# Expert weight loads issued by ScalarE instead of SyncE, and the expert tile ahead of the router in the draining steps of a fused perceiver block

## The chip, the core and the metric

One of the eight cores of a Trainium2 chip runs the program. The metric is device time in microseconds (us), of which a median of several runs is given. A profiled execution has a time of its own and a span, which runs from the first to the last instruction that the profiler saw.

## What is computed

The input is x with 64 sequences of 32 tokens and 256 channels, and a context of 64 x 257 x 256, all float32. Three blocks follow each other, each added to x:

```python
x = x + xattn(layernorm(x), ctx, ...)   # attention over the context and the own 32 keys, LoRA weights
x = x + attn(layernorm(x), ...)         # RWKV: a scan over time, then a mixture of 8 experts, top 2
x = x + ffn(layernorm(x), ...)          # GEGLU: one shared expert and 8 experts, top 1

# the mixture of the second block, ei = layernorm of its stream, shifted = ei one token later
probs = softmax(ei @ router_w); top 2 of 8, weights renormalised
xk = ei * mk + shifted * (1 - mk);  xr = ei * mr + shifted * (1 - mr)
out_e = sigmoid(xr @ eWr[e]) * (square(relu(xk @ eWk[e])) @ eWv[e])
```

eWk is 8 x 256 x 512, eWv 8 x 512 x 256, eWr 8 x 256 x 256: 4, 4 and 2 MB.

## The kernel before

The 2048 tokens are cut into G = 16 chunks of 128 (four sequences each). One software pipeline of STEPS = 25 steps, written out by hand, takes the chunks through the cross attention, the time mixing and the routing. In step s the attention works on chunk s, the time mixing begins on chunk s-3, the norm after it and the router's scores are those of chunk g = s-7, and the counting and listing of its tokens by expert is that of chunk s-8 on VectorE and s-9 on GpSimd. Each engine has its own function with its own order of the work inside a step: `mix_sync` (SyncE, only DMAs), `mix_pool` (GpSimd), `mix_tensor`, `mix_scalar` and `mix_vector`. They meet through semaphores alone, and an engine runs its list strictly in order. From step 16 on no attention chunk is left, so the steps get shorter: these are the draining steps.

The mixture of experts works on NT1 = 39 tiles of 128 token places of one expert each. Its first TA = 12 tiles need the lists of the first CUT = 10 chunks alone (`tile_map_a`, lines 1322 to 1347, in step 18), so the mixture begins at step MOE_AT = 20, inside the pipeline: each engine calls `moe(s - MOE_AT)` as the last thing of the steps 20 to 24, and alone after them. For a tile, SyncE fetches the list of its tokens (`moe_pick`, line 336: a DMA of 4 bytes to each of 128 partitions), GpSimd gathers the rows (`gather`, line 347, which waits for that list; the first three gathers stand at the end of step 19), TensorE turns them (`turned`, line 391), ScalarE copies them and the expert's eWk (`copies`, line 451), VectorE mixes (`mixed`, line 529), and TensorE multiplies (`hidden`, `receptance`, `down`). In the steps 20 to 22 the router still has the chunks 13 to 15: `router(g)` of TensorE (line 907), whose scores `router(g)` of ScalarE copies (line 1142) and VectorE's `largest` (line 1293) reads in the step after. On both engines the router stands ahead of the expert tile.

SyncE's list is the longest of the DMA lists. For each chunk `store_normed` (line 577) waits until GpSimd's `normed` (line 738) has the rows, and stores them to HBM by five DMAs: one of 128 rows of 1 KB, and one for each sequence of 31 rows of 1 KB, moved down by one token. Behind the stores of the steps 16, 17 and 18 SyncE issues the expert weights by `load_k`, `load_v` and `load_r` (lines 584 to 595). Their rows are 2 KB for eWk and 1 KB for the others:

| step | issued | rows |
|---|---|---|
| 16 | eWk of experts 0 to 5, eWr of 0 to 5 | 1536, 1536 |
| 17 | eWk of 6 and 7, eWv of 0 to 4 | 512, 2560 |
| 18 | eWv of 5 to 7, eWr of 6 and 7 | 1536, 512 |

Then comes the store of step 19 (chunk 12) and, behind it, `moe_pick` of the first 12 tiles. The weights overwrite the buffers of the attention (`arena_a`, `xz`), hence the waits in front of them. ScalarE's list has DMAs too: the context rows (`load_values`, line 1038) until step 13, and later the experts' results (`store`, line 474).

Of ScalarE's step, the parts on which the change bears are these, in order: `scaled_in`, `norm_out(g)` (line 1098, it feeds TensorE's `normed_T` and GpSimd's `normed`), `exponents`, `norm_T(g)` (line 1104), `copy_in`, `gate_exp` (line 1134), `router(g)` (line 1144), `softmax`, `load_values`, `moe`. Of TensorE's: `keys`, `turned`, `project_mix`, `normed_T(g)` (line 842), `ranks` (lines 977 to 979), `values`, `receptance`, `router(g)` (lines 912 and 914), `moe` (lines 397, 408, 423, 436).

Of the kernel before, what the change touches and what calls it, by code (L numbers as in the profile page):

```python
# [5 lines left out]
P = 128  # L6
# [54 lines left out]
def perceiver_block(nc, x_in, ctx_n, ctx_t, w_att, lora, early_in, late_in, w_mix,  # L61
                    eWk, eWv, eWr, w1s, w2s, w3s, W1, W2, W3, Wg, out):
    BATCH, S, D = x_in.shape
    KD = D // P
# [19 lines left out]
    with cx, nc.allow_non_contiguous_dma(reason="per-channel vectors, one element a partition"):  # L84
# [305 lines left out]
        def moe_tensor(pe):  # L390
# [36 lines left out]
            def down(n):  # L427
                e = pe.value_load(expert1[0:1, n:n + 1], min_val=0, max_val=E - 1)
                if n == 0:
                    pe.wait_ge(dv_ev, G)  # L430
                    pe.wait_ge(ld_moe[3], 16)
                    pe.wait_ge(ld_moe[4], 16)
                pe.wait_ge(m_dsq, n + 1)
                need(pe, m_dy, n)
                for f in range(FKC):
                    last = nc.tensor.matmul(bMY[:, 0:D], hT[:, n % 2, f * P:(f + 1) * P],  # L436
                                            ewv_sb[:, e, f * D:(f + 1) * D], start=f == 0, stop=f == FKC - 1)
                last.then_inc(m_py, 1)
# [11 lines left out]
        def moe_scalar(act):  # L450
            def copies(n):
                if n == 0:
                    act.wait_ge(pe_z, G)
                    act.wait_ge(pe_r, G)
                    act.wait_ge(dv_x1, G)
                    act.wait_ge(ld_moe[2], 16)
                    act.wait_ge(ld_moe[3], 16)
                mapped(act, n)
                act.wait_ge(m_pa, n + 1)
                need(act, m_dx, n - 1)  # L460
                nc.scalar.activation(prevT[:, n % 2], bMT[:, 0:KD * P], ACT.Copy).then_inc(m_ap, 1)
                e = act.value_load(expert1[0:1, n:n + 1], min_val=0, max_val=E - 1)
                need(act, m_ph, n - 1)
                nc.scalar.activation(wk_e[:, n % 2], ewk_sb[:, e], ACT.Copy).then_inc(m_awk, 1)  # L464
# [102 lines left out]
        def mix_sync(sp):  # L567
# [9 lines left out]
            def store_normed(n):  # L577
                sp.wait_ge(po_ei, n + 1)
                sp.dma_start(rows_e[n * P:(n + 1) * P, D:2 * D], ei[:, n % EI]).then_inc(ei_out[n % EI], 16)
                for j in range(BG):  # L580
                    r = n * P + j * S
                    sp.dma_start(rows_e[r + 1:r + S, 0:D], ei[j * S:j * S + S - 1, n % EI]).then_inc(ei_out[n % EI], 16)

            def load_k(lo, hi, i):
                sp.dma_start(ewk_sb[:, lo:hi].rearrange("p e (k f) -> p e k f", k=KD),
                             eWk[lo:hi].rearrange("e (k p) f -> p e k f", p=P)).then_inc(ld_moe[i], 16)

            def load_v(lo, hi, i):
                sp.dma_start(ewv_sb[:, lo:hi].rearrange("p e (k f) -> p e k f", k=FKC),
                             eWv[lo:hi].rearrange("e (k p) f -> p e k f", p=P)).then_inc(ld_moe[i], 16)  # L590

            def load_r(lo, hi, i):
                sp.wait_ge(dv_x1, 2 * hi)
                sp.dma_start(ewr_sb[:, lo:hi].rearrange("p e (k f) -> p e k f", k=KD),
                             eWr[lo:hi].rearrange("e (k p) f -> p e k f", p=P)).then_inc(ld_moe[i], 16)
            load_x(0)
            sp.dma_start(w_T.rearrange("p i k o -> p (i k o)"), w_att).then_inc(ld_w, 16)
            load_keys(0)
# [9 lines left out]
            for s in range(STEPS):  # L608
                n, g = s + N3, live(s - LAG - 4)
                if n in (5, 8):  # L610
                    load_x(3 if n == 5 else 4)
                if n < G:
                    load_keys(n)
                if s == 0:
                    sp.wait_ge(po_mix, 1)
                    sp.dma_start(rows_e.rearrange("(b s) d -> b s d", s=S)[:, 0, 0:D], zero_rows[:]).then_inc(zero_out, 16)
                    sp.dma_start(tab_e.rearrange("(p f) o -> p (f o)", p=P), zero_tab[:]).then_inc(zero_tab_out, 16)
                if g is not None:
                    store_normed(g)
                if s == G:  # L620
                    sp.wait_ge(pe_s, G)
                    load_k(0, 6, 2)
                    load_r(0, 6, 0)
                if s == G + 1:
                    sp.wait_ge(dv_o, G)
                    load_k(6, E, 3)
                    load_v(0, 5, 3)
                if s == G + 2:
                    sp.wait_ge(dv_x1, G)
                    load_v(5, E, 4)  # L630
                    load_r(6, E, 1)
                if s == MOE_AT - 1:
                    moe_pick(sp, range(TA))
            sp.dma_start(r2_w[:], Wg.rearrange("(k p) e -> p k e", p=P)).then_inc(ld_s, 16)
# [163 lines left out]
        def mix_tensor(pe):  # L798
# [192 lines left out]
            for s in range(STEPS):  # L991
# [30 lines left out]
                    scores(a)  # L1022
                if s == LAG - 1:
                    router_bias()
                if g is not None:
                    router(g)
                if s == STEPS - 1:
                    totals()
                if s >= MOE_AT:
                    moe(s - MOE_AT)  # L1030
            for m in range(STEPS - MOE_AT, MSTEPS):
                moe(m)

        def mix_scalar(act):
# [6 lines left out]
            for n in range(N3):  # L1041
                load_values(n)
            nc.scalar.preload_act_table(ACT.Exp)

            def hidden(n):
                act.wait_ge(pe_h, n + 1)
# [101 lines left out]
            for s in range(STEPS):  # L1148
# [23 lines left out]
                    hidden(s + 1)  # L1172
                if s == LAG - 1:
                    router_bias()
                if g is not None:
                    router(g)
                if a is not None:
                    softmax(a)
                if N3 <= s + 2 < G:
                    load_values(s + 2)  # L1180
                if s >= MOE_AT:
                    moe(s - MOE_AT)
            for m in range(STEPS - MOE_AT, MSTEPS):
                moe(m)

# [920 lines left out]
```

## Time and profile before

| | |
|---|---|
| median of 3 runs | 1017.66 us (1012.83 to 1019.77) |
| the profiled execution | 1014.11 us |
| its span | 1012.3 us |
| TensorE, matmuls, busy share of the span | 89% |
| VectorE, ScalarE, GpSimd | 42%, 29%, 31% |
| granted TensorE clock, mean over the span | 0.948 of full |
| pipeline of 25 steps | about 0 to 350 us |

Times in the rows are microseconds from the start of the span. A row of the timeline gives start, duration, engine, line, operation, what it writes from what, the shapes, and in brackets how long the engine was idle before it and what released it. "SPq" and "ACTq" rows are DMA issues of SyncE and ScalarE: their duration is that for which the issuing engine's list was held, not that of the transfer. A released-by in brackets is inferred from semaphores.

### The profile page before, as it was taken

The page shows a single profiled execution, that of the slowest core. Times are in us where ns is not written, and L with a number is a line of the kernel's source. Part 1 is how long each engine was busy: PE and PEld are TensorE (multiplying, and loading weights), DVE is VectorE, ACT ScalarE, POOL GpSimd, SP SyncE. Part 2 cuts the span into 40 slices and gives each one's busy share as a digit, 9 for nine tenths or more (in the row PEclk, how much of TensorE's full clock was granted, in tenths as well). Part 3 has the DMA queues.
Part 4 walks back from the last instruction along what each step waited for, and adds up shares of the span by engine and source line. Part 5 has one row for each costly group of instructions (what it writes and reads, how often), then busy time and mean ns, then how long its engine had stood idle before and what let it go on. Part 6 is the DMA issues. An engine that isn't in the chain of part 4 may idle for free. (4 is left out here: it accounts for less than half of the span.)

```text
span 1012.3 us, 19824 instructions
## 1 busy us (share of the span) xinstructions
PE 898.9 (89%) x6726; PEld 815.5 (81%) x6726; DVE 424.4 (42%) x1173; ACT 294.3 (29%) x665; POOL 308.9 (31%) x547
## 2 busy tenths in 40 slices
PE   5799999999723898999995999995999999999994
PEld 4577787888722788999984999994899999999993
DVE  2346766767842556555542333336111111111113
ACT  1345555545412444544531111110111111111110
POOL 1823456656515422343203322220210100100006
PEclk8899999999875899999997999997999999999998
DMA  9844545652862232325311111110699898899715
GB/s 349 260 176 163 186 121 173 149 118 38 219 216 55 64 77 67 90 85 182 111 43 58 48 32 32 31 47 11 232 347 324 298 330 317 299 310 328 260 59 166
DMA packets 100417, 163.75 MB, mean 162 GB/s; under 512 B 12488, under 2 KB 78664, under 8 KB 98152
## 3 DMA queue, kind: packets, MB, share of 16 engines
q1 hardware_dynamic: 81392, 115.82, 35.6%
q0 software_dynamic: 7552, 19.56, 7.7%
q10 hardware_dynamic: 11392, 27.34, 7.2%
q8 instruction: 46, 0.75, 0.3%
q14 instruction: 35, 0.29, 0.1%
HBM read 146.08 MB, written 16.60 MB: 161 GB/s over the span
## 5 line engine op out<-in xcount | busy, mean ns | idle before, releaser
L1697 PEld LDWEIGHTS bank<-zT_f,we 128*128 128x128 f32 x1472 | 167.9, 192 | 1.9 <-ACT zT_f L1985 0.7
L1697 PE MATMUL bank<-zT_f,we 128*128 128x128 f32 x1472 | 168.2, 275 | 0.5 <-ACT zT_f L1985 0.5
L1714 DVE TENSOR_TENSOR hT_f<-bank,act_g 128x512 f32<-128x512 f32 x78 | 53.8, 691 | 227.9 <-PE bank L1697 208.2
L1706 ACT ACTIVATE act_g<-bank 128x512 f32<-128x512 f32 x78 | 46.6, 597 | 320.8 <-PE bank L1697 320.8
L1697 PE MATMUL bank<-zT_c,a_x 128*128 128x128 f32 x1024 | 121.3, 280 | 0.3 <-PEq L1527 0.3
L1697 PEld LDWEIGHTS bank<-zT_c,a_x 128*128 128x128 f32 x1024 | 119.1, 196 | 0.8 <-issue 0.7
L863 PE MATMUL bank<-arena_b,mixed_w 128*128 128x128 f32 x768 | 94.2, 281 | 0.0
L863 PEld LDWEIGHTS bank<-arena_b,mixed_w 128*128 128x128 f32 x768 | 91.9, 197 | 1.1 <-issue 0.4
L1721 PE MATMUL bank<-we,hT_f 128*128 128x256 f32 x368 | 83.2, 379 | 0.0
L408 PE MATMUL bank<-arena_b,arena_a 128*128 128x128 f32 x624 | 79.1, 282 | 2.6 <-DVE hT L546 2.6
L408 PEld LDWEIGHTS bank<-arena_b,arena_a 128*128 128x128 f32 x624 | 75.8, 198 | 3.0 <-DVE arena_b L538 3.0
L1721 PEld LDWEIGHTS bank<-we,hT_f 128*128 128x128 f32 x368 | 68.1, 190 | 8.3
L436 PE MATMUL bank<-arena_a,hT 128*128 x312 | 73.8, 379 | 0.7 <-DVE arena_a L552 0.7
L1721 PE MATMUL bank<-mixed_w,hT_f 128*128 128x256 f32 x256 | 61.5, 395 | 5.8 <-DVE hT_f L1714 5.8
L436 PEld LDWEIGHTS bank<-arena_a,hT 128*128 128x128 f32 x312 | 59.2, 190 | 9.1 <-issue 1.1
L1926 POOL COPY pick_f<-table 128x1 uint32 (+1 forms) x23 | 4.3, 186 | 186.3 <-PE bank L1947 159.0
L1721 PEld LDWEIGHTS bank<-mixed_w,hT_f 128*128 128x128 f32 x256 | 49.7, 200 | 13.2 <-DVE hT_f L1714 6.5
L538 DVE SCALAR_TENSOR_TENSOR arena_b<-arena_b,mu_e 128x128 f32<-128x128 f32 x156 | 45.2, 352 | 6.5 <-issue 6.3
L358 POOL COPY mu_e<-late 128x4 f32 x39 | 7.3, 187 | 126.1 <-DVE arena_b L538 101.4
L464 ACT ACTIVATE arena_a<-arena_a 128x1024 f32 x39 | 41.3, 1059 | 10.3 <-issue 10.3
L360 POOL DMA_INDIRECT arena_a<-rows_e,pick x39 | 38.3, 983 | 18.1 <-issue 18.1
L423 PE MATMUL bank<-xz,arena_b 128*128 x156 | 40.7, 384 | 0.0
(279 smaller groups left out, 1304.5 us busy)
## 6 DMA issues: line engine op xcount, KB each, us to landing
we<-in_W_dram SPq DMA_DIRECT2D x69, 1024.0 KB, 7.5
arena_a<-in_ctx_n_dram ACTq DMA_DIRECT2D x16, 1152.0 KB, 8.3
arena_a<-in_ctx_t_dram SPq DMA_DIRECT2D x16, 1028.0 KB, 9.7
rows_y<-arena_a ACTq DMA_DIRECT2D x39, 128.0 KB, 1.7
arena_a<-in_eWk_dram SPq DMA_DIRECT2D x1, 3072.0 KB, 19.8
rows_f<-yr ACTq DMA_DIRECT2D x23, 128.0 KB, 6.1
arena_a<-in_eWv_dram SPq DMA_DIRECT2D x1, 2560.0 KB, 18.7
rows_e<-arena_b SPq DMA_DIRECT2D x16, 128.0 KB
```

What stands on the lines that cost most here:

```text
L358: nc.gpsimd.tensor_copy(mu_e[:, n % NM], cm_mu[:, :, e]).then_inc(m_mu, 1)
L360: nc.gpsimd.indirect_dma_start(out=pair[:, n % NM], out_offset=None, in_=rows, in_offset=bass.IndirectOffsetOnAxis(ap=pick[:, n], axis=0)) ...
L408: last = nc.tensor.matmul(bMH[:, f * P:(f + 1) * P], wk_e[:, n % 2, k * FK + f * P:k * FK + (f + 1) * P], xk[:, n % 2, k * P:(k + 1) * P], ...
L423: last = nc.tensor.matmul(bMR[:, 0:D], xr[:, n % 2, k * P:(k + 1) * P], ewr_sb[:, e, k * D:(k + 1) * D], start=k == 0, stop=k == KD - 1)
L436: last = nc.tensor.matmul(bMY[:, 0:D], hT[:, n % 2, f * P:(f + 1) * P], ewv_sb[:, e, f * D:(f + 1) * D], start=f == 0, stop=f == FKC - 1)
L464: nc.scalar.activation(wk_e[:, n % 2], ewk_sb[:, e], ACT.Copy).then_inc(m_awk, 1)
L538: last = nc.vector.scalar_tensor_tensor(o[:, n % 2, h], diffT[:, n % 2, h], mu_e[:, n % NM, i, k:k + 1], prevT[:, n % 2, h], ALU.mult, ALU ...
L863: last = nc.tensor.matmul(of_seq(bank[:, m * P:(m + 1) * P]), mixed_w[:, i, k, h, m * P:(m + 1) * P], xn[n % 2][:, k, :, 1 - h:1 - h + S], ...
L1697: last = nc.tensor.matmul(bank[half][:, f * P:(f + 1) * P], w12[:, i, k, col0:col0 + P], zT[:, k], start=k == 0, stop=k == KD - 1)
L1706: nc.scalar.activation(act_g[:, half], bU[half][:], ACT.Gelu).then_inc(self.ac_g, 1)
L1714: nc.vector.tensor_tensor(hT[:, parity, half * HH:(half + 1) * HH].rearrange("p f t -> p (f t)"), bG[half][:], act_g[:, half], ALU.mult).t ...
L1721: last = nc.tensor.matmul(bY[parity][:, 0:D], hT[:, parity, f], w3[:, f], start=f == 0, stop=f == HC - 1)
```

## The change

The three load functions move from `mix_sync` to `mix_scalar`, and their calls to the end of ScalarE's steps 16, 17 and 18. The 1.5 MB of eWr for experts 0 to 5 moves from step 16 to step 17. In the steps 20 to 24 `moe` goes ahead of `router(g)` (and of `totals`) on TensorE and ahead of `router(g)` on ScalarE. Since two loads on one semaphore (ld_moe[3]) are meant to be both waited for, the two waits on it now ask for 32 where they asked for 16.

```diff
@@ moe_tensor.down and moe_scalar.copies, n == 0
-                    pe.wait_ge(ld_moe[3], 16)
+                    pe.wait_ge(ld_moe[3], 32)
...
-                    act.wait_ge(ld_moe[3], 16)
+                    act.wait_ge(ld_moe[3], 32)
@@ mix_sync
-            def load_k(lo, hi, i):
...
-                if s == G:
-                    sp.wait_ge(pe_s, G)
-                    load_k(0, 6, 2)
-                    load_r(0, 6, 0)
-                if s == G + 1:
-                    sp.wait_ge(dv_o, G)
-                    load_k(6, E, 3)
-                    load_v(0, 5, 3)
-                if s == G + 2:
-                    sp.wait_ge(dv_x1, G)
-                    load_v(5, E, 4)
-                    load_r(6, E, 1)
@@ mix_tensor, the loop over the steps
+                if s >= MOE_AT:
+                    moe(s - MOE_AT)
                 if g is not None:
                     router(g)
                 if s == STEPS - 1:
                     totals()
-                if s >= MOE_AT:
-                    moe(s - MOE_AT)
@@ mix_scalar (load_k, load_v and load_r as above, with act for sp)
+                if s >= MOE_AT:
+                    moe(s - MOE_AT)
                 if g is not None:
                     router(g)
                 if a is not None:
                     softmax(a)
                 if N3 <= s + 2 < G:
                     load_values(s + 2)
-                if s >= MOE_AT:
-                    moe(s - MOE_AT)
+                if s == G:
+                    act.wait_ge(pe_s, G)
+                    load_k(0, 6, 2)
+                if s == G + 1:
+                    act.wait_ge(dv_o, G)
+                    load_k(6, E, 3)
+                    load_v(0, 5, 3)
+                    load_r(0, 6, 0)
+                if s == G + 2:
+                    act.wait_ge(dv_x1, G)
+                    load_v(5, E, 4)
+                    load_r(6, E, 1)
```

## Rows read from the trace of the kernel before

**Rows 1.** The page's first part: busy time of each engine, whole span.

```profile
PE 898.9 (89%) x6726; PEld 815.5 (81%) x6726; DVE 424.4 (42%) x1173; ACT 294.3 (29%) x665; POOL 308.9 (31%) x547
```

**Rows 2.** Busy time by stretch; the last three columns: granted clock, DMA share, GB/s.

```profile
277.00:286.00 9.00, 7.90 (x63) 7.25 (x62) 8.20 (x23) 4.19 (x12) 4.57 (x6) 1.00 1.10 354
292.00:302.00 10.00, 0.00 (x0) 0.00 (x0) 0.00 (x0) 0.00 (x0) 0.00 (x0) 0.50 0.69 229
303.00:305.00 2.00, 0.00 (x0) 0.00 (x0) 0.00 (x0) 0.00 (x0) 0.00 (x0) 0.50 0.12 24
```

**Rows 3.** Who waited for whom, 240 to 345 us: total, times, longest.

```profile
POOL mu_e L358 <- DMA pick<-tab_e: 24.6, 1, 24.6
```

**Rows 4.** Timeline of GpSimd: end of step 19, the first gather, a later one.

```profile
282.72 0.64 POOL L743 TENSOR_TENSOR arena_b<-arena_b,late 128x256 f32<-128x256 f32 x1
...
308.13 0.18 POOL L358 COPY mu_e<-late 128x4 f32 x1 [24.62 <-DMA pick<-tab_e]
...
330.83 0.18 POOL L358 COPY mu_e<-late 128x4 f32 x1 [2.58 <-DVE arena_b L538]
```

**Rows 5.** Timeline of SyncE's DMA issues, steps 16 to 19.

```profile
249.18 7.57 SPq L594 DMA_DIRECT2D xz<-in_eWr_dram  x1
...
272.96 3.85 SPq L589 DMA_DIRECT2D arena_a<-in_eWv_dram  x1
276.85 7.79 SPq L579 DMA_DIRECT2D rows_e<-arena_b  x1
...
291.15 3.85 SPq L594 DMA_DIRECT2D xz<-in_eWr_dram  x1
295.05 1.27 SPq L579 DMA_DIRECT2D rows_e<-arena_b  x1
...
302.46 12.53 SPq L344 DMA_DIRECT2D pick<-tab_e  x12
```

**Rows 6.** DMAs by line: the lists' landing after issue, all 39.

```profile
DMA to landing us min/median/max: 1.9/2.1/5.5
```

**Rows 7.** DMA issues of ScalarE for the context rows, ns min/median/max.

```profile
L1040 ACTq DMA_DIRECT2D arena_a<-in_ctx_n_dram x16: 334/335/574, 1.8 to 209.3; - x16
```

**Rows 8.** DMA issues by line, 240 to 305 us: KB each, us to landing.

```profile
arena_a<-in_eWv_dram SPq DMA_DIRECT2D x1, 2560.0 KB, 18.7
...
xz<-in_eWr_dram SPq DMA_DIRECT2D x1, 512.0 KB, 11.1
```

**Rows 9.** Timeline of ScalarE around the ends of the steps 17 and 18.

```profile
265.13 0.16 ACT L1144 ACTIVATE logits<-bank 128x8 f32<-128x8 f32 x1
...
265.88 0.60 ACT L1098 ACTIVATE arena_b<-a_x,rs 128x256 f32<-128x256 f32 x1
...
276.69 0.16 ACT L1144 ACTIVATE logits<-bank 128x8 f32<-128x8 f32 x1
276.75 0.59 ACT L1098 ACTIVATE arena_b<-a_x,rs 128x256 f32<-128x256 f32 x1
```

**Rows 10.** Timeline of TensorE in step 18.

```profile
266.53 0.44 PE L842 MATMUL bank<-ident,arena_b 128*128 128x128 f32 x2 [0.89 <-ACT arena_b L1098]
269.06 0.17 PE L977 MATMUL bank<-earlier,ones_m 128*128 128x8 bf16 x1 [2.09 <-DVE arena_b L1246]
```

**Rows 11.** Timeline of all engines, steps 21 to 23.

```profile
324.22 0.60 ACT L1098 ACTIVATE arena_b<-a_x,rs 128x256 f32<-128x256 f32 x1 [3.90 <-POOL rs L732]
...
325.43 0.17 PE L979 MATMUL bank<-earlier,ones_m 128*128 128x8 bf16 x1
...
326.57 1.02 PE L914 MATMUL bank<-r_wg,arena_b 128*128 128x8 f32 x4
...
327.45 1.09 PE L397 MATMUL bank<-ident,arena_a 128*128 128x128 f32 x4
...
333.39 0.39 ACT L472 ACTIVATE sig<-bank 128x256 f32<-128x256 f32 x1 [0.80 <-PE bank L423]
333.41 0.17 DVE L1295 MAX8 top<-logits 128x8 f32<-128x8 f32 x1
...
344.60 0.18 PE L978 MATMUL bank<-mask,before_m 128*128 128x8 bf16 x1 [1.65 <-DVE mask L1307]
```

More of the change, by code:

```diff
@@ L582, in store_normed @@
                     sp.dma_start(rows_e[r + 1:r + S, 0:D], ei[j * S:j * S + S - 1, n % EI]).then_inc(ei_out[n % EI], 16)
-            def load_k(lo, hi, i):
[L585 to L595, printed above, removed]
             load_x(0)
@@ L1043, in mix_scalar, with load_k, load_v, load_r @@
             nc.scalar.preload_act_table(ACT.Exp)
+            def load_k(lo, hi, i):
+                act.dma_start(ewk_sb[:, lo:hi].rearrange("p e (k f) -> p e k f", k=KD),
+                             eWk[lo:hi].rearrange("e (k p) f -> p e k f", p=P)).then_inc(ld_moe[i], 16)
+            def load_v(lo, hi, i):
+                act.dma_start(ewv_sb[:, lo:hi].rearrange("p e (k f) -> p e k f", k=FKC),
+                             eWv[lo:hi].rearrange("e (k p) f -> p e k f", p=P)).then_inc(ld_moe[i], 16)
+            def load_r(lo, hi, i):
+                act.wait_ge(dv_x1, 2 * hi)
+                act.dma_start(ewr_sb[:, lo:hi].rearrange("p e (k f) -> p e k f", k=KD),
+                             eWr[lo:hi].rearrange("e (k p) f -> p e k f", p=P)).then_inc(ld_moe[i], 16)
             def hidden(n):
```

## The prediction

> **What bounds the kernel now.** I read the page first: TensorE is busy 89% of the span [rows 1], so time can be won only where it stands still or runs at the low clock. The busy time by stretch finds the one large hole in the pipeline. Up to 286 us every engine works (TensorE 7.90 of 9 us). From 292 to 302 us no engine does anything, and only the DMAs run, at 229 GB/s. From 303 to 305 us they run at 24 GB/s [rows 2]. The waits name who holds the hole: GpSimd stood 24.6 us before the first gather, for the list of the first tile's tokens [rows 3], from its last work at 283.36 to 308.13 us [rows 4]. All the others are behind GpSimd: the norm of the next chunk (line 728 on) comes after the gathers in its list.
>
> Why is the list late? SyncE's timeline answers. From 249 us on its list is almost without a gap made of issues that hold it for microseconds: 7.57, 3.85, 7.79, 3.85 [rows 5]. Chunk 12's rows were ready at 283.36 us [rows 4], its store was issued at 295.05 and the first list at 302.46 [rows 5]. The list landed 5.5 us later, against a median of 2.1 [rows 6]. The pattern of the long issues is that an issue is held until the rows of the DMA in front of it have been handed over. The issue at 249.18 stands behind 1536 rows and takes 7.57. That at 272.96 stands behind 512 rows: 3.85. That at 276.85 stands behind 2560: 7.79. That at 291.15 stands behind 1536: 3.85. That at 295.05 stands behind 512: 1.27 [rows 5]. So a big DMA costs little by itself, but it costs the engine that wants to issue the next one. The 5.5 us have another cause: the four stores of 31 rows move at 24 GB/s [rows 2], and 124 KB need 5.3 us at that rate. The list is behind them in SyncE's queue.
>
> **The loads leave SyncE.** Its stores are then issued when the rows are ready and the lists right behind them. If nothing else moved, the store of chunk 12 would go out at 283.4 instead of 295.05, 11.7 us earlier. But the loads go into ScalarE's list, and that list is worked on.
>
> Step 16: one load at the end, 0.4 us (ScalarE's own issues take 0.335 [rows 7]), with nothing behind it. It is issued at about 253 us, 4 us later than now, and has 12 us until the next. I cost it at nothing: the next that ScalarE does is followed by a wait for VectorE anyway.
>
> Step 17: three loads behind line 1144 (265.13 + 0.16 [rows 9]). The wait for dv_o is long met, and so is that for dv_x1 at 12. eWk of 6 and 7: 0.4. eWv behind its 512 rows: between 1.27 and 3.85 [rows 5]. eWr behind the 2560 rows of eWv: 7.79 [rows 5], or by 2.5 ns a row (3.85 us for 1536) 6.4. I take the pair that has the same DMAs, 3.85 and 7.79: together 12.0 us, bounds 8.1 and, with 7.57 for the first of them, 15.8. ScalarE is then free at 277.3 instead of 265.3. Queued behind: `scaled_in`, `norm_out(11)` and, behind those, `exponents`. `norm_out(11)` ends at 278.5 instead of 266.48 [rows 9]. TensorE's line 842 waits for it, and the ranks behind it move from 269.06 to 279.0, since 2.09 us of idle time there are used up [rows 10]: 9.9 us of shift. VectorE's tile map waits for the ranks, TensorE's values, receptance and router follow, and line 1144 of step 18 moves from 276.69 [rows 9] to 286.7.
>
> Step 18: two loads. eWv of 5 to 7: 0.4, since the rows in front of it have been handed over by then. eWr of 6 and 7 behind its 1536 rows: 3.85 [rows 5], bounds 2 and 7.57. ScalarE is free at 291.1 us, and `norm_out(12)`, now at 276.75 [rows 9], ends at 291.7. GpSimd's `normed(12)` is two operations of 0.65 (the second in [rows 4]), so the rows are ready at 293.1 us, against 283.36 now.
>
> From there to the gather: five stores, then the list. Now it is 308.13 - 295.05 = 13.1 us from the first store to the gather [rows 4, 5], with the last 2048 rows of weights and chunk 11's stores in front in the same queue. Alone it is 5.3 us for the stores and 2.1 for the list [rows 2, 6], 7.4. The last weights, issued at 291, still share the DMA engines for a part of it (now such a load lands 11.1 us after issue [rows 8]). I take 10.0, about the middle. The gather begins at 303.2 us instead of 308.13: 4.9 us earlier. With every term at its low end (8.1, 2.4, 7.4) it is 13 us earlier. With 15.8, 8.0 and 13.1 it is 6 us later. So the hole of 24.6 us shrinks to about 10, and stalls of 16 us that were not there take most of the difference.
>
> Are the weights there in time? eWk 0 to 5 and the DMAs on ld_moe[3] are needed by ScalarE's copies in step 20, some 14 us after 291. The eWr of 6 and 7 lands at 291 + 11 = 302 us, before the first receptance, which needs the gather and 15 us more. The 32 on ld_moe[3] costs nothing, for both loads are issued in step 17.
>
> A rule of the Trainium skill speaks for a better outcome. "DMA: Bandwidth & Descriptors", section "Issuing engines are not separate DMA queues", says that issuing from several engines saves only the sequencer's time to issue, which is usually small relative to the DMA. The trace has it otherwise for SyncE: 7.79 us to issue behind a 2560 KB load that lands 18.7 us after issue [rows 8] is not small. Were it small on ScalarE, the sum would be that of the first rival below.
>
> **The expert tile in front of the router, steps 20 to 24.** `router` exists in three of them only (20 to 22). Moved on both engines it counts once, because ScalarE's copy waits for TensorE. In step 21 the loop that sets the pace is: GpSimd's norm, `norm_out` at 324.22, line 842, ranks until 325.60, router until 327.59, then the turning of the tile at 327.45, ScalarE's and VectorE's part, and GpSimd's gather at 330.83, behind which the next norm stands [rows 4, 11]. With the tile in front the turning starts at 325.6: 1.85 us earlier, in step 20 about the same, so 3.6 us by the end of step 21. Then it is given back in part. The scores of chunk 14 come behind `hidden` and `receptance`, ScalarE's copy of them behind line 472 (333.39, or 329.8 when moved [rows 11]), that is at about 331.8 us, and two things stand behind it: `norm_out(15)` on ScalarE and VectorE's line 1295, now at 333.41 [rows 11]. Gain there 1.6 to 2.1. In step 23 TensorE's ranks wait for VectorE's mask anyway (1.65 us idle at 344.60 [rows 11]), and that chain is held by the late scores. I take 2.2 us for the whole, bounds 5.5 (three times 1.85) and -2 (a router of 1.5 us waited for in the open once, with nothing won in step 22).
>
> **The sum.** 4.9 + 2.2 = 7.1 us less. The profiled execution would be at 1014.11 - 7.1 = 1007.0. It stands 3.5 us under the median of the runs, so I state 1017.66 - 7.1 = 1010.5 us. Behind step 24 nothing has a fixed hour: the tiles follow each other and the shift is carried to the end.
>
> **The rivals.**
>
> A. ScalarE is not held. Then `normed(12)` ends at 283.4, the store goes out at once and the list takes 7.4 to 13.1, here 10: gather at 293.4, 14.7 us earlier; with 2.2, 16.9: 1000.8 us. For it: all ScalarE's issues so far took 0.335 us, at most 0.57 [rows 7]. Against it: those had 128 rows each, a twentieth of eWv's, and SyncE's own long issues stand only behind big loads [rows 5].
>
> B. The gain is eaten: ScalarE's stalls are 20 us in all or the list needs its 13.1 us again, since stores and weights still share the DMA engines. Gather at 308, and 1 us won in the drain: 1016.5 us. For it: from 277 to 286 us the DMAs moved 354 GB/s at a share above 1 [rows 2], so the loads themselves are near what they can be, and 4608 rows in one go at step 17 are more than ever stood together.
>
> C. Slower: the stalls of ScalarE become the bound. The work in front of `norm_out(12)` is shifted by step 17's stall less 2.1, and step 18's stall is added whole. If eWr's issue in step 17 takes 7.57 + 7.79 + 0.4 = 15.8 and the one in step 18 with 1536 rows of eWr still in front 3.85 + 7.57 = 11.4, the rows are ready at 293.1 + 3.8 + 7.2 = 304.1 us, the gather is at 314.1, 6 us later, and with 2.2 won in the drain 1021.5 us. It decides from 16.3 + 4.9 + 2.2 = 23.4 us of stalls in steps 17 and 18 together. Against it: SyncE's issues behind the same loads took 3.85 + 7.79 = 11.6 us for step 17 and 3.85 + 1.27 = 5.1 for step 18 [rows 5].
>
> **How the numbers follow.** Forecast 0.60, A 0.18, B 0.14, C 0.08. The forecast alone spans 1004 to 1016 us. A reaches below 1000 with the list at its 7.4, C up to 1022. I cut both tails: 1000 to 1019. About 1% is what a measurement of this kernel tells from no change, 10.2 us. Below 1007.5 lie A and a quarter of the forecast: 0.33. Above 1027.8 lies what is worse than C's price: 0.04. The rest, 0.63, is within 1%.
>
> **What would show it.** Right: DMA issues of ScalarE of some 4 and 8 us at 265 to 277, one of about 4 at 287 to 291, and line 1098 of step 18 some 12 us later than 265.88. SyncE's issues under 2 us, and its first list at about 296. GpSimd's wait for the list about 9 us instead of 24.6, the gather at 303. Line 397 ahead of line 912 in steps 20 to 22, with the step from gather to gather near 8 us at first instead of 9.7. Wrong: ScalarE's issues all under 1 us (A), the gather at 308 (B), or after it (C); a wait of ScalarE for a weight load in step 20; or line 1295 in step 22 later than 333.41 - 4.9.

## The result, and the profile after

The changed kernel takes 1020.48 us (median of 12 runs, 1018.00 to 1024.73), the kernel before 1015.92 us beside it (12 runs, 1012.61 to 1020.46). The ratio is 1.0042, with a 95% interval of 1.0021 to 1.0062. So it is slower by 4.6 us, outside my range of 1000 to 1019 and on the other side of the forecast of 1010.5 us. A change of under 1% was the case to which the prediction gave 0.63, and this is one; its direction was forecast wrongly. One run of experiment e8 below took 1208.69 us at a granted clock of 0.735 where its others had 0.954 to 0.959; it is left out of e8's figures, no other kernel had such a run, and its cause is open.

The profiled execution took 1024.73 us, with a span of 1023.0 us, 10.7 us above that of before. It is the slowest of the twelve, so the size of each term below is read from its trace and the size of the whole from the medians.

The page's first part shows the same matmuls, busy 4 us longer than in [rows 1]:

```profile
PE 903.0 (88%) x6726; PEld 819.0 (80%) x6726; DVE 426.2 (42%) x1173; ACT 293.9 (29%) x665; POOL 308.7 (30%) x547
```

**The loads on ScalarE.** The timeline of ScalarE, steps 17 and 18 (L1086 is the line that was 1098, L1132 was 1144), answers to [rows 9]:

```profile
265.12 0.38 ACTq L1021 DMA_DIRECT2D arena_a<-in_eWk_dram  x1
...
265.53 0.53 ACTq L1025 DMA_DIRECT2D arena_a<-in_eWv_dram  x1
266.10 15.56 ACTq L1030 DMA_DIRECT2D xz<-in_eWr_dram  x1
281.76 0.81 ACT L1100 ACTIVATE arena_b<-bank,late 128x128 f32<-128x128 f32 x2 [16.13 <-issue]
282.46 0.59 ACT L1086 ACTIVATE arena_b<-a_x,rs 128x256 f32<-128x256 f32 x1
...
290.87 0.97 ACTq L1030 DMA_DIRECT2D xz<-in_eWr_dram  x1
291.97 0.60 ACT L1086 ACTIVATE arena_b<-a_x,rs 128x256 f32<-128x256 f32 x1 [1.26 <-issue]
```

ScalarE's list stands for 15.56 us at one instruction: the issue of eWr, behind the 2560 rows of eWv. Its norm in front of step 18's work (chunk 11) starts at 282.46 where it started at 265.88. The DMAs are slow for most of that time (busy time by stretch; last three columns: granted clock, DMA share, GB/s; the other rows are used further down):

```profile
274.00:284.00 10.00, 0.89 (x6) 0.83 (x7) 0.09 (x1) 2.17 (x6) 0.78 (x2) 0.50 1.05 176
...
300.00:303.00 3.00, 0.16 (x1) 0.00 (x0) 2.60 (x11) 0.00 (x0) 0.00 (x0) 0.77 0.08 5
306.00:312.00 6.00, 0.00 (x0) 0.00 (x0) 0.00 (x0) 0.00 (x0) 0.00 (x0) 0.50 0.12 23
356.00:362.00 6.00, 1.62 (x8) 0.94 (x6) 4.64 (x18) 0.26 (x1) 0.05 (x1) 0.80 0.04 13
362.00:368.00 6.00, 5.48 (x25) 5.24 (x25) 2.87 (x8) 2.17 (x4) 2.29 (x4) 0.63 0.34 89
```

From 274 to 284 us they are as busy as in the first row of [rows 2] and move half as much: 176 GB/s, not 354. And TensorE, which worked 7.90 of 9 us there, works 0.89 of 10. Such a slow stretch is not new with the change: in the kernel before the DMAs move 153 GB/s from 262 to 266 us, at a share of 1.15.

**The stores and the first list.** SyncE's issues, steps 18 to 20, answer to [rows 5]:

```profile
284.51 0.34 SPq L579 DMA_DIRECT2D rows_e<-arena_b  x1
284.90 4.27 SPq L582 DMA_DIRECT2D rows_e<-arena_b  x4
297.24 0.34 SPq L579 DMA_DIRECT2D rows_e<-arena_b  x1
297.62 6.65 SPq L582 DMA_DIRECT2D rows_e<-arena_b  x4
305.37 12.85 SPq L344 DMA_DIRECT2D pick<-tab_e  x12
```

SyncE is free now: the store of chunk 12 goes out as soon as GpSimd has the rows. But these come at 297.2 us, later than the 295.05 at which the held SyncE stored them before. The first list is issued at 305.37 and not at 302.46. GpSimd's timeline, the end of step 19 and the first gathers, answers to [rows 4]:

```profile
296.57 0.64 POOL L718 TENSOR_TENSOR arena_b<-arena_b,late 128x256 f32<-128x256 f32 x1
...
312.43 0.18 POOL L358 COPY mu_e<-late 128x4 f32 x1 [15.06 <-DMA pick<-tab_e]
...
324.03 0.18 POOL L358 COPY mu_e<-late 128x4 f32 x1 [0.91 <-DVE arena_b L538]
...
332.13 0.18 POOL L358 COPY mu_e<-late 128x4 f32 x1 [0.90 <-DVE arena_b L538]
```

The wait for the list fell from 24.62 to 15.06 us, and the gather still begins 4.3 us later (312.43 against 308.13). A shorter wait is no gain where it begins later. Two gathers later 332.13 stands against 330.83: the draining steps win time, and by the gather at 348.05 us (347.69 before) the shift is down from 4.3 to 0.4.

**The totals behind the expert tile.** Then comes the loss that I had not priced. The timeline of step 24 and the tile after it:

```profile
356.37 0.17 PE L959 MATMUL bank<-earlier,ones_m 128*128 128x8 bf16 x1
356.60 0.29 DVE L1353 TENSOR_TENSOR scratch<-bank,tile_lo 128x128 f32<-128x128 f32 x1 [4.42 <-PE bank L959]
...
360.62 1.09 PE L397 MATMUL bank<-ident,arena_a 128*128 128x128 f32 x4 [4.08 <-DVE arena_b L531]
...
361.95 0.19 POOL L358 COPY mu_e<-late 128x4 f32 x1 [9.64 <-DVE arena_b L538]
...
362.52 3.75 PE L408 MATMUL bank<-arena_b,arena_a 128*128 128x128 f32 x16 [0.82 <-DVE hT L546]
```

And the same operations before:

```profile
349.55 0.17 PE L984 MATMUL bank<-earlier,ones_m 128*128 128x8 bf16 x1
...
350.56 0.29 DVE L1353 TENSOR_TENSOR scratch<-bank,tile_lo 128x128 f32<-128x128 f32 x1 [0.38 <-issue]
...
354.58 0.63 PE L397 MATMUL bank<-ident,arena_a 128*128 128x128 f32 x4
...
355.91 0.19 POOL L358 COPY mu_e<-late 128x4 f32 x1 [3.95 <-DVE arena_b L538]
...
356.48 2.02 PE L408 MATMUL bank<-arena_b,arena_a 128*128 128x128 f32 x16 [1.27 <-DVE hT L546]
```

`totals` is one matmul of 0.17 us. VectorE's map of all 39 tiles (lines 1353 on) waits for it, and the mixing of the next tile stands behind that map on VectorE. With the whole of `moe` in front, VectorE waits 4.42 us with nothing to do. TensorE then waits 4.08 for VectorE, and GpSimd 9.64. The shift jumps from 0.4 to 6.0 us (361.95 against 355.91). After so little work the clock is low: mean granted 0.80, then 0.63 in the rows by stretch above, and 0.50 from 362.5 to 366.2 us. The 16 matmuls of line 408 take 3.75 us there and not 2.02. One more group of the same 16, at 411.01 us, takes 3.57 against 2.02 at 403.08. Both together bring the shift to 9.5 us, and there it stays to the last part of the kernel. That the second group is owed to the totals is not shown: e3 below, which doesn't wait for them, has a group of 3.75 us at 403.94 too, and e4 has none.

### The profile page after: what moved, and what is told of

Read it like the earlier page. It is cut to its first block and busy times, and to the rows that moved or that the text cites. A ratio compares the mean times of both kernels' runs of the same rounds, so it can differ in the third digit from the quotient of the medians.

```text
span 1023.0 us, 19824 instructions
## 1 busy us (share of the span) xinstructions
PE 903.0 (88%) x6726; PEld 819.0 (80%) x6726; DVE 426.2 (42%) x1173; ACT 293.9 (29%) x665; POOL 308.7 (30%) x547
## 3 DMA queue, kind: packets, MB, share of 16 engines
q10 hardware_dynamic: 19680, 37.82, 10.7%
## 5 line engine op out<-in xcount | busy, mean ns | idle before, releaser
L408 PE MATMUL bank<-arena_b,arena_a 128*128 128x128 f32 x624 | 83.0, 291 | 2.1 <-DVE hT L546 2.1
L408 PEld LDWEIGHTS bank<-arena_b,arena_a 128*128 128x128 f32 x624 | 79.7, 207 | 2.7 <-DVE arena_b L538 2.7
L817 PE MATMUL bank<-ident,arena_b 128*128 128x128 f32 x32 | 7.3, 315 | 41.5 <-ACT arena_b L1086 41.5
## 6 DMA issues: line engine op xcount, KB each, us to landing
arena_a<-in_eWk_dram ACTq DMA_DIRECT2D x1, 3072.0 KB, 15.8
```

The lines of the kernel that those rows point to most:

```text
L408: last = nc.tensor.matmul(bMH[:, f * P:(f + 1) * P], wk_e[:, n % 2, k * FK + f * P:k * FK + (f + 1) * P], xk[:, n % 2, k * P:(k + 1) * P], ...
L817: last = nc.tensor.transpose(bT[:, k * P:(k + 1) * P], z3[:, n % 2, k * P:(k + 1) * P], ident[:])
```

## The experiments

Each time stands beside runs of the kernel before on the same chip. "Gather" is the start of the first gather in the profiled execution, "map" that of VectorE's first step of the tile map. A profiled execution is one of many, and it can lie some microseconds off the median (e3's lies 6.5 us above); the ratios come from all runs.

| kernel | time | before | ratio (95%) | gather | map |
|---|---|---|---|---|---|
| before | | | 1 | 308.1 | 350.6 |
| changed | 1020.48 | 1015.92 | 1.0042 (1.0021 to 1.0062) | 312.4 | 356.6 |
| e1 loads only | 1016.46 | 1014.98 | 1.0016 (0.9990 to 1.0041) | 311.2 | 354.9 |
| e2 order only | 1018.52 | 1014.98 | 1.0026 (1.0010 to 1.0041) | 306.3 | 350.6 |
| e3 changed, totals first | 1013.03 | 1014.98 | 0.9976 (0.9948 to 1.0003) | 311.1 | 351.4 |
| e4 order only, totals first | 1011.96 | 1014.98 | 0.9972 (0.9951 to 0.9993) | 307.1 | 346.0 |
| e5 e4, last two loads in step 19 | 1011.40 | 1013.75 | 0.9974 (0.9956 to 0.9992) | 305.7 | 344.5 |
| e6 e3, five loads in step 19 | 1007.31 | 1013.75 | 0.9940 (0.9918 to 0.9962) | 294.3 | 340.6 |
| e7 e3, eWr before eWv | 1012.78 | 1013.75 | 0.9974 (0.9953 to 0.9994) | 310.2 | 348.8 |
| e8 e4, stores of 16 and 15 rows | 1002.18 | 1013.75 | 0.9865 (0.9841 to 0.9888) | 303.1 | 342.0 |
| e9 e8, four loads in step 19 | 999.60 | 1022.03 | 0.9799 (0.9755 to 0.9844) | 294.5 | 331.5 |
| e10 e3, stores of 16 and 15 rows | 1006.78 | 1022.03 | 0.9850 (0.9810 to 0.9891) | 301.0 | 341.2 |
| e11 before, stores of 16 and 15 rows | 1011.03 | 1022.03 | 0.9885 (0.9843 to 0.9927) | 302.2 | 346.2 |

**The change in its parts.** e1 keeps the loads on ScalarE and the order of before; e2 keeps the loads on SyncE and takes the new order, totals behind.

```diff
# e1, against the changed kernel, on TensorE (and the same on ScalarE)
-                if s >= MOE_AT:
-                    moe(s - MOE_AT)
                 if g is not None:
                     router(g)
                 if s == STEPS - 1:
                     totals()
+                if s >= MOE_AT:
+                    moe(s - MOE_AT)
```

Expected of e1:

> The loads on ScalarE, the order of the draining steps as it was. Theory (two parts): ScalarE is held about 15 us by its third load of step 17 again, the first gather comes 4.3 us later than before (312 us), and nothing wins it back, so the kernel is 3 to 6 us slower than before. Rival (the loads are the whole loss): the first gather as late, and more is lost after 350 us, so it is as slow as the changed kernel or slower, some 4 to 10 us over before, and the tile map is as late in it as there.

Expected of e2:

> The draining steps in the new order, the loads on SyncE as before. Theory: the steps 20 to 23 are 3.5 to 4 us shorter together, then the last sum of the counts, which now stands behind the tile of step 24 on TensorE, makes VectorE wait 4 to 5 us and costs 6 us, with TensorE at the low clock for one product after it (1.5 to 2 us more): in all 2 to 5 us slower than before. Rival: the order wins 4 us and keeps them, 4 us faster.

e1: the loads alone move the gather by 3.1 us to the late side and cost 1.6 us, not distinguishable from none. ScalarE's issue of eWr held it 13.69 us here. I had expected 3 to 6 us of loss; the trace has 5.5 us of span (1017.8 against 1012.3), the twelve runs do not. e2: the new order alone, which I had priced at 2.2 us of gain, costs 2.6. Its trace gains 5.6 us by the gather at 342 us and has lost all of it at the map (350.63 against 350.56, after the same 4.42 us of wait for the totals).

**The totals alone.** e3 is the changed kernel, e4 is e2, each with two lines moved:

```diff
+                if s == STEPS - 1:
+                    totals()
                 if s >= MOE_AT:
                     moe(s - MOE_AT)
                 if g is not None:
                     router(g)
-                if s == STEPS - 1:
-                    totals()
```

Expected of e3:

> The changed kernel with that last sum in front of the tile in step 24 again. Theory: VectorE's wait of 4.4 us and TensorE's of 4.1 us at 356 to 361 us are gone, the kernel is 5 to 8 us faster than the changed one and about equal to before (0 to +1 us; the gather is late by 4.3, the steps 20 to 23 win 3.9). Rival (loads are the whole loss): no more than 1 us faster than the changed kernel.

Expected of e4:

> The loads on SyncE as before, the tile in front of the router, the last sum in front of the tile. Theory: 3 to 5 us faster than before, the best of the four. Rival (the order's gain is given back behind step 24, because the scores come late): within 1 us of before.

From the changed kernel to e3 the ratio falls from 1.0042 to 0.9976, and from e2 to e4 from 1.0026 to 0.9972: 6.7 and 5.5 us for the place of one matmul of 0.17 us, once with the loads on ScalarE and once with them on SyncE. In the traces the map comes 5.2 and 4.7 us earlier. The map in e3's trace waits for nothing, and ScalarE is held as long as ever:

```profile
267.19 13.78 ACTq L1030 DMA_DIRECT2D xz<-in_eWr_dram  x1
```

```profile
351.41 0.29 DVE L1353 TENSOR_TENSOR scratch<-bank,tile_lo 128x128 f32<-128x128 f32 x1 [0.38 <-issue]
```

In e4 the gain of the drain is kept. TensorE goes from the totals into the tile without a gap, and line 408 runs at full clock:

```profile
344.94 0.17 PE L984 MATMUL bank<-earlier,ones_m 128*128 128x8 bf16 x1
344.96 0.63 PE L397 MATMUL bank<-ident,arena_a 128*128 128x128 f32 x4
345.44 1.95 PE L408 MATMUL bank<-arena_b,arena_a 128*128 128x128 f32 x16
```

e3 has lost a little of it: TensorE, busy without a gap, has a mean granted clock of 0.56 from 345.5 to 349 us, and the gather at that place comes 1.7 us later than at e4's pace (356.76 after 346.88, against 351.30 after 343.08).

This settles the sign of the result. The two other terms, the loads and the tile ahead of the router, nearly cancel: e3's ratio has an interval of 0.9948 to 1.0003, so it is level with the kernel before or slightly faster.

**Where the loads stand.** e5 is e4 with the loads of step 18 alone given to ScalarE, at the end of step 19, when ScalarE has nothing behind it until the gather. e6 is e3 with all loads but the first there. e7 is e3 with the 1536 rows of eWr ahead of the 2560 of eWv.

```diff
# e5, against e4 (e6 does it for all loads but eWk 0 to 5)
-                if s == G + 2:
-                    sp.wait_ge(dv_x1, G)
-                    load_v(5, E, 4)
-                    load_r(6, E, 1)
...
+                if s == G + 3:
+                    act.wait_ge(dv_x1, G)
+                    load_v(5, E, 4)
+                    load_r(6, E, 1)
# e7, against e3
-                    load_v(0, 5, 3)
                     load_r(0, 6, 0)
+                    load_v(0, 5, 3)
```

Expected of e5:

> The version with the loads on SyncE, the tile in front of the router and the last sum in front of the tile (e4), with the two loads of step 18 alone issued by ScalarE, at the end of its step 19, where it stands still for over 20 us. Theory (the store of chunk 12 and the list are late because of the issues and rows in front of them in SyncE's queue): the store goes out at 290 to 291 us instead of 294.4, ScalarE shows no stall in steps 18 and 19, the gather comes at 299 to 303 us instead of 307.1, the kernel is 4 to 8 us faster than that version. Rival (the rows share the DMA engines, whoever issues): gather within 1.5 us of 307 and no gain.

Expected of e6:

> The changed kernel with the last sum first (e3), and with five of its six loads at the end of ScalarE's step 19, the 2560 rows second to last. Theory (what a load costs is the work queued behind the issue): ScalarE is held for 10 to 20 us there and nothing waits for it, steps 18 and 19 have no stall, the rows of chunk 12 are ready at 283 to 284 us, and the gather comes at 291 to 297 us instead of 311, the kernel 10 to 18 us faster than e3, unless ScalarE's hold lasts beyond the gather or the weights land after 315 us. Rival (a long hold is paid anywhere, since all 13 MB have to come first): the gather at 305 us or later, or ScalarE waits for the weights in step 20, and less than 5 us are won.

Expected of e7:

> e3 with the 1536 rows of eWr ahead of the 2560 of eWv in step 17. Theory (an issue is held until the rows in front of it are handed over): the second issue is short, the third is held 4 to 9 us instead of 14 to 16, ScalarE's work goes on at about 273 us instead of 281, the first issue of step 18 is held in its turn for 2 to 6 us behind the 2560 rows, and the gather comes 1 to 5 us earlier than in e3 (311). Rival (the hold is that of the bytes in all, or of a slow stretch of the DMAs that comes anyway): ScalarE goes on at 279 us or later.

e5: the store of chunk 12 goes out at 287.7 us, 6.7 earlier than in e4, and the gather starts only 1.4 earlier. SyncE is then held by the small stores themselves, in place of the loads:

```profile
287.71 3.07 SPq L579 DMA_DIRECT2D rows_e<-arena_b  x1
290.82 7.43 SPq L582 DMA_DIRECT2D rows_e<-arena_b  x4
299.35 10.79 SPq L344 DMA_DIRECT2D pick<-tab_e  x10
```

The packets of the trace say the same: from 296 to 300 us the small stores and ScalarE's loads move 10 to 13 rows per us each, and from 300 us the stores alone move 23 to 24. The time is e4's (0.9974 against 0.9972), as the rival had it and not my theory, which gave 4 to 8 us. So from here the stores of 31 rows are the limit.

e6: with no load but that of step 16 on the way the list goes out at 284.96 us and the gather is at 294.3, 16.8 us earlier than in e3. Of that, 10.8 us are left at the map, since ScalarE is now held into the first tile, and the weights land late (timeline of ScalarE). The runs show less: the ratio is 0.36 points below e3's, 3.7 us, where I had expected 10 to 18. The spans of the two profiled executions differ by 14.0 us, but e3's lies 6.5 us above its median and e6's 1.7 below, and e3's trace has the two slow stretches named above.

```profile
301.95 0.60 ACT L1086 ACTIVATE arena_b<-a_x,rs 128x256 f32<-128x256 f32 x1 [18.04 <-issue]
...
311.22 0.38 ACT L461 ACTIVATE arena_b<-bank 128x256 f32<-128x256 f32 x1 [6.21 <-DMA arena_a<-in_eWv_dram]
```

e7: the hold changes its place and stays. The three issues of step 17 take 0.38, 1.84 and 5.71 us, the pair of step 18 then 5.46 and 10.30. ScalarE goes on at 272.9 us, as expected, and gains nothing by it: the store of chunk 12 is at 298.9, 2.4 us later than in e3, the gather 0.9 us earlier, and the ratio is e3's (0.9974 and 0.9976).

**The stores.** e8 is e4 with each store of 31 rows cut in two (and the count that the readers wait for raised to match); e11 is the kernel before with that alone, e10 is e3 with it.

```diff
-        OUT_PER = 16 * (1 + BG)
+        OUT_PER = 16 * (1 + 2 * BG)
...
-                    sp.dma_start(rows_e[r + 1:r + S, 0:D], ei[j * S:j * S + S - 1, n % EI]).then_inc(ei_out[n % EI], 16)
+                    for lo, hi in ((0, S // 2), (S // 2, S - 1)):
+                        sp.dma_start(rows_e[r + 1 + lo:r + 1 + hi, 0:D], ei[j * S + lo:j * S + hi, n % EI]).then_inc(ei_out[n % EI], 16)
```

Expected of e8:

> e4 with each store of 31 rows cut into one of 16 and one of 15 rows (nine DMAs a chunk instead of five). Theory (a DMA of 31 rows moves at 24 GB/s and holds up all that stands behind it in SyncE's queue, weights and lists): the last store and the list land 4 to 9 us earlier, first gather at 298 to 303 us instead of 307.1, and 4 to 8 us are won. Rival (nine issues cost more than five, the rate of the small ones is no matter): no gain or a loss of 1 to 3 us.

SyncE's issues of e8 in the steps 18 to 20:

```profile
273.08 11.38 SPq L579 DMA_DIRECT2D rows_e<-arena_b  x1
284.50 3.94 SPq L583 DMA_DIRECT2D rows_e<-arena_b  x8
288.48 0.39 SPq L590 DMA_DIRECT2D arena_a<-in_eWv_dram  x1
288.92 4.93 SPq L595 DMA_DIRECT2D xz<-in_eWr_dram  x1
293.89 0.95 SPq L579 DMA_DIRECT2D rows_e<-arena_b  x1
294.89 3.58 SPq L583 DMA_DIRECT2D rows_e<-arena_b  x8
299.58 10.70 SPq L344 DMA_DIRECT2D pick<-tab_e  x10
```

Eight stores take 3.58 us to issue where four took 4.56 in e4, the list lands 3.4 us after its issue and not 5.5, and the gather is 4.0 us earlier than in e4. The DMAs from 298 to 300 us, which moved 72 GB/s in e4 (there the weights were through and only small stores were left from 299 us on), are at their full rate:

```profile
298.00:300.00 2.00, 0.00 (x0) 0.00 (x0) 0.00 (x0) 0.00 (x0) 0.00 (x0) 0.50 1.08 346
```

The Trainium skill has a rule for it, in "DMA: Bandwidth & Descriptors", section "Why a DMA increments its semaphore by 16 and not by 1": a transfer is spread over as many DMA engines as the largest number up to 16 that divides the slowest dimension of both its sides. Here that dimension is the rows, which makes one engine for 31 rows and 16 and 15 for the halves. The trace agrees for the 31 rows: from 303 us on the packets of the kernel before follow each other one by one, a row of 1 KB every 0.042 us, which is the 24 GB/s of [rows 2].

From e4 to e8 the ratio falls by 1.07 points, 10.9 us (by the medians, 1002.18 of 1013.75 and 1011.96 of 1014.98, it would be 8.5), more than the 4 to 8 I had expected and more than the 4.0 us at the gather and 3.9 at the map. A good part of the difference is which executions were profiled: e4's was 1.1 us below its median and e8's 4.2 above. Of what is left I can show no place.

Expected of e11:

> The kernel before with nothing but the stores of 31 rows cut into 16 and 15 rows. Theory: the gather moves from 308 to about 304 and the shift is carried to the end: 4 to 6 us less, ratio 0.9945 +- 0.002; with the order of the drain and the totals first 8 to 10 less was seen, so 3 to 4 of these are the order's. Rival, that short stores gain at other places too (all stores of all 16 chunks are issued faster): over 7 us less.

Expected of e10:

> The changed kernel with the totals ahead of the expert tile and the stores of 16 and 15 rows. ScalarE issues the weights in the steps 16 to 18. It and the run with the short stores alone (loads on SyncE) differ only in who issues the weights and when. Theory that the hold moves with the loads: ScalarE is held 14 to 16 us at 265, store of chunk 12 at 296 as in the changed kernel, but the list behind it takes 3 us instead of 7 and the gather is at about 305 to 307 against 303.1: 1005 to 1008 us, 2 to 4 over the loads on SyncE. Rival, that ScalarE's holds matter only through the slow stores: gather at 303, 1003.6 us. If short stores gain less than 4 us here, the loads share the DMA engines with them.

e11: the stores alone gain 1.15% (interval 0.73 to 1.57), 11.7 us, the rival's size. The trace doesn't bear it out: the gather is 5.9 us earlier and the map 4.3, and the span of 1012.9 us, at a granted clock of 0.942 (0.948 before), is that of before; this execution is 3.6 us above e11's median. The runs of the kernel before beside e9 to e11 had a median of 1022.03 us, 6 to 8 above those of the other groups of runs, so times of different groups of runs are compared by their ratios alone, and of e11's gain I take the 4 to 6 us of the trace as shown, and the rest as open. e10 is level with e8: 0.9850 against 0.9865. With short stores ScalarE was held only 7.50 us at the same issue that held it 15.56, and the gather was at 301.0 us, 2 us before e8's; neither my theory (14 to 16 us, gather at 305 to 307) nor its rival had that. So the hold of ScalarE is no constant of the change (e10's timeline of ScalarE):

```profile
267.22 7.50 ACTq L1031 DMA_DIRECT2D xz<-in_eWr_dram  x1
```

**The best version.** e9 is e8 with the loads of the steps 17 and 18 issued by ScalarE at the end of step 19, small ones first (and 32 for both waits on ld_moe[3]).

```diff
+                if s == G + 3:
+                    act.wait_ge(dv_o, G)
+                    act.wait_ge(dv_x1, G)
+                    load_k(6, E, 3)
+                    load_r(6, E, 1)
+                    load_v(0, 5, 3)
+                    load_v(5, E, 4)
```

Expected of e9:

> Stores of 16 and 15 rows, expert tile first, totals ahead of it; the loads of the steps 17 and 18 issued by ScalarE at the end of step 19 (eWk of 6 and 7, eWr of 6 and 7, eWv of 0 to 4, eWv of 5 to 7); those of step 16 stay with SyncE. Two limits were found so far: SyncE held by the loads until the store of chunk 12 (11.38 and 4.93 us in the run with the short stores), and 5 us of small stores ahead of the lists. Theory that both limits add: nothing holds SyncE, store of chunk 12 at 282, list landed at 287, first gather at 287 to 290 against 303.1 with the short stores alone. But the weights land only at about 302 (5 MB at 350 GB/s from 285), so ScalarE's copies wait for them and most of the gain stops there: 1001 us, 2 to 3 us less than with the short stores alone. Rival: the weights are the end of it in both, so the time is that of the short stores alone, 1003.6 +- 1.5.

Timelines of SyncE, ScalarE and GpSimd in e9:

```profile
281.76 0.34 SPq L579 DMA_DIRECT2D rows_e<-arena_b  x1
282.14 3.57 SPq L583 DMA_DIRECT2D rows_e<-arena_b  x8
286.82 13.38 SPq L344 DMA_DIRECT2D pick<-tab_e  x12
```

```profile
286.43 8.86 ACTq L1043 DMA_DIRECT2D arena_a<-in_eWv_dram  x2
300.35 0.60 ACT L1104 ACTIVATE arena_b<-a_x,rs 128x256 f32<-128x256 f32 x1 [14.70 <-POOL rs L725]
```

```profile
294.53 0.18 POOL L358 COPY mu_e<-late 128x4 f32 x1 [12.64 <-DMA pick<-tab_e]
```

The hold of ScalarE ends at 295.3 us, 5 us before its next work, and no wait of ScalarE for a weight is left. So my expectation that the weights stop the gain was wrong: the gather is 8.6 us earlier than in e8, the map 10.5, the span 9.8 (994.8). The ratio is 0.9799 (0.9755 to 0.9844): 2.0% faster than the kernel before (1.6 to 2.5%), and by the two ratios, an estimate since they come from different groups of runs, 2.4% faster than the changed one (0.9799 / 1.0042 = 0.9758). By the traces it is 17.5 us of span against before (1012.3 - 994.8), 1.7%.

## Why the prediction was wrong

**The step that failed: "`router` exists in three of them only (20 to 22)", and with it the sum's last sentence, "Behind step 24 nothing has a fixed hour".** The diff puts `moe` ahead of `totals` in step 24 as well. I priced the router's move and never the totals'. Behind step 24 the map of all tiles does have an hour: it waits for the totals, and VectorE's next tile for the map. Measured: 6.7 us (changed to e3) and 5.5 us (e2 to e4), for a term that the sum had at nothing. In the changed kernel's trace the waits shift the gather by 5.6 us (0.4 to 6.0) and the first group of matmuls at the low clock adds 1.7; how the 6.7 and 5.5 of the medians divide is not shown. With the totals in front the kernel was 0.9976 of the one before (0.9948 to 1.0003), on the forecast side or level, and inside my range.

**ScalarE's hold in step 17: 12.0 us, bounds 8.1 to 15.8; it was 16.5** (0.38 + 0.53 + 15.56). The engine was held where the prediction said, and the size was off. I took SyncE's two holds behind the same loads, at 354 GB/s; here the 2560 rows went at 176 for some eight of those microseconds. The low rate alone is not the reason: e10 has a like stretch (190 GB/s from 275 to 281 us), but its hold had ended before it. By the packets, 2340 of eWv's 2560 rows had moved when the hold of 15.56 us ended and 946 when e10's of 7.50 did, so "until the rows in front are handed over" is not the same as until they are moved, and what ends a hold stays open. Also, the holds are not one for each pair of DMAs: eWv behind 512 rows took 0.53 and not 3.85, and the next issue took all of it. In step 18 it was 1.35 us and not 4.25, since by then the rows in front were gone. Both together, 17.8 us, are near my 16.3.

**Rows of chunk 12 ready at 293.1; it was 297.2.** I followed the chain over `norm_out(12)`. That was over at 292.6. GpSimd was later for its own reasons: VectorE's line 1264 let it go at 292.23, and then its norm and two issues of the list stood ahead (0.83 + 1.09 + 1.20 us and the gaps).

**From the store to the gather: 10.0 us, bounds 7.4 to 13.1; it was 15.2** (297.24 to 312.43). I had counted the four small stores of one chunk, 5.3 us at 24 GB/s. What I had not priced is that the small stores share their one engine with the weights of the other queue. The packets of the changed kernel's trace show it, by queue. Three of chunk 11's stores of 31 rows take 2.63, 2.33 and 2.63 us (289.6 to 297.3 us), with rows of ScalarE's loads in between; in the kernel before, where both stand in one queue, such a store takes 1.32. The fourth ends only at 302.4. From 299 to 304 us hardly more than one packet at a time is under way, now of SyncE's queue and now of ScalarE's, and three rows of ScalarE's loads take 0.68, 1.77 and 1.13 us where the others take 0.046: hence the 5 GB/s from 300 to 303 us. Why these three are so long stays open. The 124 rows of chunk 12's four stores then move from 305.0 to 311.6 us, 6.6 us and not 5.3, since until 307.9 half of the 23 GB/s is ScalarE's. On SyncE this shows as the last of the four issues, held 5.35 us of the 6.65. So leaving SyncE's list did not take the loads out of the way of its stores; it let them run side by side on the one engine that a store of 31 rows uses. e5, e8 and e11 show the limit of the small stores from three sides. So the gather came 4.3 us later and not 4.9 earlier.

**The tile in front of the router: 2.2 us won, bounds 5.5 and -2; it was 3.9** until the gather at 348 us in the changed kernel (4.3 down to 0.4), 3.8 from e2's gather to 341 us (1.8 early, then 5.6). Line 397 now starts at 328.37, right behind the ranks. The mechanism was right, the give-back smaller than I took it.

**The rivals.** C, slower, got the side, and the price by chance: it put 6 us on the gather and won 2.2 in the drain, where 4.3 and 3.9 were measured, nearly nothing together. Its point of decision, 23.4 us of stalls, was not reached, and the gather was late all the same, through the stores. A needed a ScalarE that isn't held; placed at the end of step 19, where the hold has cover, e6 and e9 reach its gather (294), though not for its reason. B, the gain eaten, is the closest to e1 and e3: gather at 311 where it said 308.

## What to carry to other kernels

Price every call that an edit moves, the one-matmul ones too: what counts is who stands behind its result, not its duration. A big load costs the engine that issues something behind it, on whichever engine that is; so the question is not only which engine to give it to but at which point that engine has nothing to do for the length of the transfer. Two queues are not two sets of DMA engines: ask which small transfers the big one will run beside. And a shorter wait in the profile says nothing before the hour at which it ends is compared.

## What the runs showed of the hardware

- An issue of a 1.5 MB load was held 15.56 us, 13.69, 13.78 and 7.50 us at the same place of four kernels. While the longest lasted the DMA engines were busy and moved half as much (176 GB/s against 354). Stretches of this kind stand in the kernel before (153 GB/s, 262 to 266 us) and in e10 after its short hold (190 GB/s, 275 to 281 us) as well; what halves the rate stays open, and so does what makes the hold short: e10 had the stores of 16 and 15 rows, but e8 with the same stores had a hold of 11.38 us on SyncE.
- A store of 31 rows of 1 KB is dearer than one of 16 and one of 15 together, at twice the number of issues: its rows move one by one, at 24 GB/s. With the halves the first gather came 4.0 us earlier (e8) and 5.9 (e11), and the ratio fell by 1.1 points in both.
- Small stores on SyncE's queue and loads on ScalarE's share a DMA engine: a store of 31 rows took 2.3 to 2.6 us beside the loads in the changed kernel, and 1.32 us in the kernel before, where both stand in SyncE's queue.
- Behind one wait of 4.08 us of TensorE the next 16 matmuls took 3.75 us instead of 2.02, at a granted clock of 0.50, on top of the wait. A second group of the same form 50 us later took 3.57 where it had taken 2.02, though nothing in its own wait had changed (1.28 us in both). e3, without the long wait, has such a group as well (3.75 us at 403.94), so what lowers the clock there is open.
